# Centring only ahead of the first transposes, rstd folded in behind them, and new orders for all engines of a retention and mixture-of-experts layer

## The reference

```python
def _layernorm(x, axis=-1, eps=1e-05):
    m = jnp.mean(x, axis=axis, keepdims=True)
    v = jnp.var(x, axis=axis, keepdims=True)
    return (x - m) / jnp.sqrt(v + eps)
# attention of x = _layernorm(x)
q = (x @ Wq.T).reshape(B, T, H, dk)
k = (x @ Wk.T).reshape(B, T, H, dk)
q, k = _apply_rotary(q, k)
v = jnp.transpose((x @ Wv.T).reshape(B, T, H, dv), (0, 2, 1, 3))
scores = jnp.einsum('bhtd,bhsd->bhts', q * dk ** (-0.5), k) * decay_mask[None]
o = jnp.transpose(jnp.einsum('bhts,bhsd->bhtd', scores, v), (0, 2, 1, 3))
rms = jax.lax.rsqrt(jnp.mean(o * o, axis=-1, keepdims=True) + EPS)
g = (x @ Wg.T).reshape(B, T, H, dv)
x = x0 + (o * rms * g_norm_w * (g * jax.nn.sigmoid(g))).reshape(B, T, H * dv) @ Wo.T
# experts, of xf = _layernorm(x) in rows
shared = jax.nn.silu(xf @ sh_up_w + sh_up_b) @ sh_down_w + sh_down_b
comb = top-2 softmax weights of xf @ gate_w.T, scaled to sum to one
h = jax.nn.silu(jnp.einsum('nd,edh->neh', xf, up_w) + up_b)
y = jnp.einsum('ned,ne->nd', jnp.einsum('neh,ehd->ned', h, down_w) + down_b, comb)
return x + y + shared
```

## Time and profile before

| | us |
|---|---|
| median of 3 runs | 142.51 (142.03 to 142.53) |
| the profiled execution | 142.45 |
| its span in the profile | 140.7 |
| TensorE busy in it | 130.8 (93%) |
| VectorE busy | 104.2 (74%) |
| ScalarE busy | 78.6 (56%) |
| GpSimd busy | 48.8 (35%) |

### The profile page before, as it was taken

The page is one execution under the profiler, slowest core; times in us unless marked ns, Lnnn a source line. Parts: engine busy times, 40 slices in busy tenths (PEclk is TensorE's granted clock), DMA queues, the critical chain, the costliest instruction groups (busy, mean ns, idle before and its releaser), DMA issues.

```text
span 140.7 us, 3363 instructions
## 1 busy us (share of the span) xinstructions
PE 130.8 (93%) x1249; PEld 103.7 (74%) x1249; DVE 104.2 (74%) x311; ACT 78.6 (56%) x138; POOL 48.8 (35%) x69
## 2 busy tenths in 40 slices
PE   5659899899999999999998999999999999999990
PEld 5549799798978988886885675776557655589990
DVE  3589999989689997998796949679443982113983
ACT  4223937955562478555659762697745864471130
POOL 5458897937372342815222804502000000000000
PEclk9977999999999999999999999999999999999999
DMA  4999910000000000097000097010197200002002
GB/s 113 296 274 317 334 68 0 5 0 5 0 5 0 2 5 0 17 320 270 2 5 0 16 317 270 2 56 19 47 276 283 75 2 0 0 0 79 0 0 75
DMA packets 8659, 12.50 MB, mean 89 GB/s; under 512 B 1298, under 2 KB 5676, under 8 KB 8644
## 3 DMA queue, kind: packets, MB, share of 16 engines
q1 hardware_dynamic: 8356, 12.10, 26.7%
q10 hardware_dynamic: 288, 0.20, 0.4%
HBM read 11.20 MB, written 1.10 MB: 87 GB/s over the span
## 4 chain that ended last, share of the span: by engine, by line
PE 72%; DVE 10%; DMA 5%; SPq 4%; ACT 3%; issue 3%; DVEq 0%
PE bY L1238 17%; PE bU L1061 8%; PE bU L1062 7%; PE bU L1063 7%; DMA UW<-upw 5%; PE bA L1135 5%; PE bA L1211 4%; PE bU L1154 3%; PE bA L1129 3%; PE bA L1105 2%; PE bM L1154 2%; PE bU L1145 2%; PE bM L1180 1%; DVE SC L724 1%; SPq L267 1%
## 5 line engine op out<-in xcount | busy, mean ns | idle before, releaser
L497 ACT ACTIVATE HB<-bU,UB 128x512 f32<-128x512 f32 x36 | 24.3, 686 | 22.0 <-PE bU L1063 21.7
L1238 PE MATMUL bY<-HG,DW 128*128 128x512 f32 x48 | 24.5, 594 | 0.0
L848 DVE TENSOR_TENSOR HG<-CB,HB 128x512 f32<-128x512 f32 x24 | 16.3, 688 | 10.9 <-ACT HB L497 10.2
L353 POOL TENSOR_TENSOR RR<-SS,NHALF 128x8 f32<-128x8 f32 x8 | 13.5, 1684 | 25.9 <-DVE SS L743 25.9
L1061 PE MATMUL bU<-XH,UWH 128*128 128x512 f32 x36 | 21.5, 597 | 0.0
L1062 PE MATMUL bU<-XL,UWH 128*128 128x512 f32 x36 | 14.2, 395 | 0.0
L1063 PE MATMUL bU<-XH,UWL 128*128 128x512 f32 x36 | 14.2, 393 | 0.0
L1061 PEld LDWEIGHTS bU<-XH,UWH 128*128 128x128 f32 x36 | 6.8, 189 | 5.5 <-issue 4.3
L1238 PEld LDWEIGHTS bY<-HG,DW 128*128 128x128 f32 x48 | 8.4, 190 | 2.5 <-issue 1.4
L724 DVE TENSOR_TENSOR SC<-bA,MASK 128x512 f32<-128x512 f32 x16 | 10.2, 679 | 0.0
L1062 PEld LDWEIGHTS bU<-XL,UWH 128*128 128x128 f32 x36 | 6.8, 190 | 3.4 <-issue 3.4
(11 more groups left out here) (180 smaller groups left out, 317.8 us busy)
## 6 DMA issues: line engine op xcount, KB each, us to landing
CB<-scratch SPq DMA_DIRECT2D x12, 512.0 KB, 5.8
ROT<-rotary_tables SPq DMA_DIRECT2D x8, 256.0 KB, 4.5
out<-OUT SPq DMA_DIRECT2D x8, 128.0 KB, 1.8
X<-x SPq DMA_DIRECT2D x7, 128.0 KB, 6.1
UW<-upw SPq DMA_DIRECT2D x1, 576.0 KB, 6.6
DW<-dnw SPq DMA_DIRECT2D x1, 576.0 KB, 5.5
W<-wqkvg SPq DMA_DIRECT2D x1, 256.0 KB, 3.7
W<-wqkvg ACTq DMA_DIRECT2D x1, 128.0 KB, 3.9
```

The costliest lines, as they stand in the source:

```text
L353: pool.tensor_tensor(RR[:, n], SS[:, n], NHALF[:, 0:2 * H], ALU.pow).then_inc(rr.sem, 1)
L497: act.activation(HB[:, k, :], bU[(g * (E + 1) + k) % 2][:, :], ACT.Silu, bias=UB[:, e:e + 1]).then_inc(hid.sem, 1)
L848: dve.tensor_tensor(HG[:, k % RING, :], CB[:, k - 1, :], HB[:, k, :], ALU.mult).then_inc(gated.sem, 1)
L1238: pe.matmul(bY[:, :], DW[:, e * P:(e + 1) * P], HB[:, 0, :] if k == 0 else HG[:, k % RING, :], start=(k == 0), stop=(k == E)).then_inc(dow ...
```

## The change

For the first two pairs VectorE's `center1` subtracts the mean only, and rstd, a factor of each row of q, k, v and gate alike, comes in behind the projections: as a scale in `values` and `gates` (ScalarE, now in two halves for these pairs), and in `rotary` and `rotate` as fused instructions with three operands (VectorE, two for each product). `NORM1` goes from 4 to 2, so the pairs of group 1 are normalised on ScalarE and need `x1_bias`. The `rotate` of the first two groups and `low_w(1)`, the low half of the V and gate weights, move from GpSimd to VectorE. The V and gate weights are loaded by ScalarE's queue behind the Q and K weights, no longer by SP's queue ahead of x, and one load of x moves ahead of the constants. Ten warm-up matmuls become seven and two, in another bank. The lists of all engines and the banks in `PLACE` are new; the sets of steps in them are otherwise the same. The diff, cut to these edits and to the first part of each list (and the last part of TensorE's):

```diff
@@ -40,22 +40,23 @@
 SLOTS = 4
 TABLES = 6
 
-NORM1, NORM2 = 4, 4
+NORM1, NORM2 = 2, 4
+
+FOLD = 2
 
...
@@ -267,13 +268,12 @@
                 sp.dma_start(dst, rotary_tables[n // 2, :, c]).then_inc(ld_rot[n].sem, 16)
 
             load_first_x(sp, 0)
-            sp.dma_start(W[:, QK:], wqkvg[:, QK:]).then_inc(ld_w[1].sem, 16)
             load_x(sp, 1)
             load_rotary(0)
             load_x(sp, 2)
             load_rotary(1)
+            load_x(sp, 3)
             sp.dma_start(CN[:, :], const).then_inc(ld_c.sem, 16)
-            load_x(sp, 3)
             load_rotary(2)
             load_rotary(3)
...
 
             rstd1(0, 0)
             rstd1(0, 1)
-            low_w(1)
             rstd1(1, 0)
             rstd1(1, 1)
             fold_norm()
-            rotate(0, 0)
             low_experts()
-            rotate(0, 1)
             rstd1(2, 0)
             rstd1(2, 1)
-            rotate(1, 0)
-            rotate(1, 1)
+            rms(0, 0)
             rstd1(3, 0)
-            rms(0, 0)
+            normalize_out(0, 0)
             rstd1(3, 1)
-            normalize_out(0, 0)
...
             load_first_x(act, 1)
             act.dma_start(W[:, 0:QK], wqkvg[:, 0:QK]).then_inc(ld_w[0].sem, 16)
+            act.dma_start(W[:, QK:], wqkvg[:, QK:]).then_inc(ld_w[1].sem, 16)
...
             def x1_norm(g, p):
-                act.wait_ge(nm1.sem, pair(g, p) - NORM1 + 1)
+                act.wait_ge(nm1.sem, pair(g, p) - max(NORM1, FOLD) + 1)
...
             def values(g, p):
                 act.wait_ge(v_ps.sem, v_ps.at(g, p))
-                act.copy(V[:, slot(g, p)].rearrange("r b n -> r (b n)"), place("proj_v", g, p)).then_inc(v_sb.sem, 1)
+                if pair(g, p) < FOLD:
+                    act.wait_ge(rs1.sem, rs1.at(g, p))
+                    for b in range(2):
+                        last = act.activation(V[:, slot(g, p), b], place("proj_v", g, p)[:, b * HV:(b + 1) * HV], ACT.Identity,
+                                              scale=RS1[:, 2 * pair(g, p) + b:2 * pair(g, p) + b + 1])
+                else:
+                    last = act.copy(V[:, slot(g, p)].rearrange("r b n -> r (b n)"), place("proj_v", g, p))
+                last.then_inc(v_sb.sem, 1)
 
             def gates(g, p):
                 act.wait_ge(g_ps.sem, g_ps.at(g, p))
                 if pair(g, p) >= SLOTS:
                     act.wait_ge(ogr.sem, ogr.at(*back(g, p, SLOTS)))
-                act.activation(SG[:, slot(g, p)].rearrange("r b n -> r (b n)"), place("proj_g", g, p), ACT.Silu).then_inc(sg.sem, 1)
+                if pair(g, p) < FOLD:
+                    act.wait_ge(rs1.sem, rs1.at(g, p))
+                    for b in range(2):
+                        last = act.activation(SG[:, slot(g, p), b], place("proj_g", g, p)[:, b * HV:(b + 1) * HV], ACT.Silu,
+                                              scale=RS1[:, 2 * pair(g, p) + b:2 * pair(g, p) + b + 1])
+                else:
+                    last = act.activation(SG[:, slot(g, p)].rearrange("r b n -> r (b n)"), place("proj_g", g, p), ACT.Silu)
+                last.then_inc(sg.sem, 1)
...
             split_w(0)
+            x1_hi(0, 0)
             split_w(1)
-            x1_hi(0, 0)
             x1_hi(0, 1)
             gates(0, 0)
+            gates(0, 1)
+            x1_norm(1, 0)
+            values(0, 0)
+            values(0, 1)
+            qk_sb(0, 0)
+            x1_hi(1, 0)
             split_experts()
-            gates(0, 1)
-            values(0, 0)
-            x1_hi(1, 0)
-            values(0, 1)
+            x1_norm(1, 1)
+            qk_sb(0, 1)
+            split_biases()
+            gates(1, 0)
             x1_hi(1, 1)
-            split_biases()
-            qk_sb(0, 0)
-            gates(1, 0)
+            squares(0, 0)
+            values(1, 0)
+            x1_norm(2, 0)
+            values(1, 1)
+            qk_sb(1, 0)
+            x1_norm(2, 1)
             gates(1, 1)
-            qk_sb(0, 1)
...
+            def center1(g, p):
+                dve.wait_ge(mv1.sem, mv1.at(g, p))
+                for b in range(2):
+                    t = g * TILES + 2 * p + b
+                    last = dve.tensor_scalar(XN1[:, g % 2, (2 * p + b) * P:(2 * p + b + 1) * P], X[:, t * P:(t + 1) * P],
+                                             MV1[:, t, 0:1], None, ALU.subtract)
+                last.then_inc(xn1.sem, 1)
...
-                dve.tensor_tensor(RA[:, p], src.rearrange("r (b n) -> r b n", b=2), cos.unsqueeze(1).to_broadcast([P, 2, QK]),
-                                  ALU.mult)
+                if pair(g, p) < FOLD:
+                    dve.wait_ge(rs1.sem, rs1.at(g, p))
+                    for b in range(2):
+                        t = 2 * pair(g, p) + b
+                        dve.scalar_tensor_tensor(out=RA[:, p, b], in0=src[:, b * QK:(b + 1) * QK], scalar=RS1[:, t:t + 1], in1=cos,
+                                                 op0=ALU.mult, op1=ALU.mult)
+                else:
+                    dve.tensor_tensor(RA[:, p], src.rearrange("r (b n) -> r b n", b=2),
+                                      cos.unsqueeze(1).to_broadcast([P, 2, QK]), ALU.mult)
...
             def rotate(g, p):
                 dve.wait_ge(rparts.sem, rparts.at(g, p))
+                if pair(g, p) < FOLD:
+                    for b in range(2):
+                        t = 2 * pair(g, p) + b
+                        last = dve.scalar_tensor_tensor(out=QKR[:, slot(g, p), b], in0=RB[:, p, b], scalar=RS1[:, t:t + 1],
+                                                        in1=RA[:, p, b], op0=ALU.mult, op1=ALU.add)
+                    last.then_inc(rot.sem, 1)
+                    return
...
             stats1(0, 0)
+            center1(0, 0)
             stats1(0, 1)
+            center1(0, 1)
+            x1_lo(0, 0)
             low_w(0)
-            normalize1(0, 0)
-            normalize1(0, 1)
-            x1_lo(0, 0)
+            low_w(1)
+            x1_lo(0, 1)
             stats1(1, 0)
-            x1_lo(0, 1)
+            rotary(0, 0)
+            x1_bias(1, 0)
             stats1(1, 1)
-            rotary(0, 0)
-            normalize1(1, 0)
-            normalize1(1, 1)
+            rotate(0, 0)
             rotary(0, 1)
+            state(0, 0)
+            rotate(0, 1)
             x1_lo(1, 0)
+            x1_bias(1, 1)
             stats1(2, 0)
+            masked(0, 0)
+            rotary(1, 0)
+            stats1(2, 1)
             x1_lo(1, 1)
-            state(0, 0)
-            stats1(2, 1)
-            rotary(1, 0)
-            masked(0, 0)
+            rotate(1, 0)
+            x1_bias(2, 0)
+            gate_out(0, 0)
+            mean_squares(0, 0)
+            x1_bias(2, 1)
+            state(0, 1)
+            stats1(3, 0)
+            masked(0, 1)
+            state(1, 0)
+            stats1(3, 1)
+            x1_lo(2, 0)
...
-                    pe.matmul(bY[:, 0:P], IDN[:, :], IDN[:, :], start=True, stop=True)
+                    pe.matmul(bA[:, 3, 0:P], IDN[:, :], IDN[:, :], start=True, stop=True)
...
             pe.wait_ge(idn.sem, 1)
-            keep_busy(10)
+            keep_busy(7)
             x1_t(0, 0)
+            keep_busy(2)
             x1_t(0, 1)
+            after(xl1, 0, 0)
             proj_qk(0, 0)
             proj_g(0, 0)
             after(xl1, 0, 1)
+            proj_g(0, 1)
             proj_qk(0, 1)
-            proj_g(0, 1)
+            after(rparts, 0, 0)
             proj_v(0, 0)
-            after(xl1, 0, 0)
+            after(sg, 0, 1)
+            proj_v(0, 1)
+            after(sg, 0, 0)
+            qk_t(0, 0)
+            after(v_sb, 0, 0)
+            state_add(0, 0)
             x1_t(1, 0)
-            proj_v(0, 1)
-            after(sg, 0, 1)
+            after(rparts, 0, 1)
+            scores(0, 0)
+            after(qkt, 0, 0)
+            qk_t(0, 1)
+            after(st, 0, 0)
+            proj_qk(1, 0)
+            after(v_sb, 0, 1)
+            proj_g(1, 0)
+            after(qkt, 0, 1)
             x1_t(1, 1)
-            qk_t(0, 0)
-            after(v_sb, 0, 1)
-            state_add(0, 0)
-            after(rparts, 0, 1)
-            proj_qk(1, 0)
+            attend(0, 0)
+            after(rparts, 1, 0)
+            proj_v(1, 0)
+            after(sg, 1, 0)
+            state_add(0, 1)
             after(xl1, 1, 1)
-            proj_g(1, 0)
-            after(v_sb, 0, 0)
-            after(sg, 0, 0)
-            scores(0, 0)
-            after(st, 0, 0)
-            proj_qk(1, 1)
-            after(rparts, 1, 0)
-            proj_g(1, 1)
-            after(sg, 1, 0)
-            qk_t(0, 1)
-            after(xl1, 1, 0)
-            state_add(0, 1)
-            attend(0, 0)
-            after(rparts, 1, 1)
-            proj_v(1, 0)
-            after(qkt, 0, 1)
             proj_v(1, 1)
-            after(sg, 1, 1)
+            after(v_sb, 1, 0)
             qk_t(1, 0)
-            after(st, 0, 1)
-            x1_t(2, 0)
...
             down_last(3, 1)
```

(11 more changed lines are left out.)

510 lines of the change are left out of this document (244 added, 266 removed), and 23 rows, old and new, of the table PLACE.

## The result

The changed kernel takes 138.70 us (median of 4 runs, 138.29 to 139.15), the kernel before 142.27 us beside it (141.86 to 142.53): a ratio of 0.975, 95% interval 0.971 to 0.980, so 3.6 us less where 1.9 were forecast. The profiled execution took 138.97 us with a span of 137.2, against 142.45 and 140.7 before. In all that follows a median takes in every execution, and a ratio leaves out those more than 1.5% above the fastest of their kernel.

The account below looks back on a forecast made before the run. VectorE and TensorE were taken to bind the attention part together. TensorE's lead of 3.0 us less a router 1.1 us later gave a gain of 1.9: 142.45 - 1.9 = 140.55 us, range 138.4 to 142.6.

Parts of the forecast that it names:

- The start: Front of the run: first projection at 6.9 us instead of 9.36, 2.4 us sooner, between 1.9 and 3.0.
- W came earlier: V and gate weights' load on ScalarE's queue: seen at 7.5 us, between 6.8 and 8.4; VectorE waits 1.25 us.
- The path to the first router: VectorE up to x2_lo(0, 1): net 5.0 us more work, there at 48.2 us; TensorE's router 1.1 us later.
- Other idle time, about 3 us: VectorE's remaining waits ahead of the first router: left unchanged, as no row says the new order has less.
- the recovered clock: TensorE's clock at the front: not counted again, since TensorE there waits for VectorE and not its own pace.
- The stretched instructions of VectorE beside GpSimd: Ahead of the first router: four normalisations and two tiny biases lose their waits beside GpSimd, 2.0 us back.
- TensorE's lead: At the first router: net 3.0 us of matmul work already issued that lay behind it before.
- new idle time: TensorE behind the router, where combine weights return by DMA: counted at nothing; its appearance would show the forecast wrong.
- The tail: End of the run: two up-projections move between down-projections, same matmuls in all; nothing, within 0.2 us.
- TensorE sets the pace, W early: Rival for the front: W seen at 6.8 us saves 0.7, less idle time 1.5 more; 138.35 us, chance 0.23.
- W late and the clock low: Rival for the front: W seen at 8.4 us, TensorE's clock falls, first projections at half rate; 142.1 us, chance 0.20.
- VectorE's new instructions stand behind GpSimd: Rival: VectorE's added SBUF instructions meet GpSimd's long ones, three or four meetings cost 3.5 us; 144.05 us, chance 0.12.

Follow-up runs that it names:

- e5: The changed kernel itself, run again unchanged beside other runs on the same chip: 138.89 us, ratio 0.976 to the kernel before.
- e7: Changed kernel with the V and gate weights' load back second on SyncE's queue: 138.48 us, ratio 0.975 to the kernel before.
- e1: Changed kernel without its nine warm-up matmuls: 139.77 us, ratio 0.980 to the kernel before.
- e4: Changed kernel with its orders, but first two pairs fully normalised by VectorE and V and gate weights loaded as before: 141.00 us, ratio 0.988 to the kernel before.
- e13: Orders alone (old normalisation and loads) with nine warm-up matmuls for seven and five for two: 139.46 us, ratio 0.980 to the kernel before.
- e2: Kernel before with twelve warm-up matmuls for ten and three more between the first two pairs' transposes: 142.22 us, ratio 0.999.
- e11: Changed kernel with rotations of pairs (1, 0) and (1, 1) and low half of V and gate weights back on GpSimd: 140.61 us, ratio 0.990 to kernel before.
- e8: Changed kernel with values(3, 1) moved ahead of transposed_out(2, 0) in ScalarE's order: 138.03 us, ratio 0.970 to the kernel before.
- e6: Changed kernel with first two pairs normalised by VectorE again, its orders and loads kept: 140.79 us, ratio 0.988 to the kernel before.
- e3: Kernel before with only the centring and later rstd for the first two pairs, their rotations on VectorE: 144.87 us, ratio 1.018.
- e10: As e3, with ScalarE's cast of the experts' up weights moved behind the high half of pair (1, 0): 142.93 us, ratio 1.002 to the kernel before.
- e9: Orders alone (old normalisation and loads) with five warm-up matmuls for two behind the first transposes: 140.29 us, ratio 0.983 to the kernel before.

## Why the prediction was right and wrong

**The start was right.** First projection 6.94 us (forecast 6.9), x for pair (0, 1) at 4.84 (4.9), low half of the first pair at 6.04 (6.2), no stretched centring. That x landed so close to the forecast is in part chance: in e5, the same kernel, its statistics start at 4.40 without a wait, and with W back on SyncE's queue (e7) x came at 5.01, 0.17 later, where the sum of the queue's bytes had up to 1.2.

**W came earlier than I took it**, seen at 6.86 us, at the lower of my two bounds (6.8) and not at 7.5, and VectorE's wait was 0.73 us and not 1.25. The shares of the two queues from 4.5 to 5.5 us in the changed kernel:

```profile
q10 hardware_dynamic: 96, 0.18, 54.7%
q1 hardware_dynamic: 105, 0.12, 44.3%
```

With rows of 2 KB ScalarE's queue got the larger share, where with rows of 1 KB it had 24.1% against 68.0. The Trainium skill (DMA: Bandwidth & Descriptors, section Queues, rings and completion order) says that each DMA engine takes turns between the queues, a packet at a time. The counts here agree, 96 packets against 105; those before don't, 90 against 296, and no run tells why. The load itself, by e7, decides nothing.

**The path to the first router is the step that failed, and with it the idle time on that path.** The sum went along VectorE, to which it gave "Other idle time, about 3 us, I leave as it is", let "TensorE's router" start at about 48.4 us behind it, and left the clock out: "the recovered clock isn't counted again, since at the front TensorE now waits for VectorE and not for its own pace". The router started at 46.85 us, 0.2 sooner than before (its first matmul was at 47.03 there) where the sum had 1.1 later. In VectorE's terms: from the first low half to the end of x2_lo(0, 1) it was busy for 34.91 of 37.75 us before and for 37.31 of 39.71 after. Its work grew by 2.4 us where the sum had 5.0 - 2.0 = 3.0. Its idle time fell from 2.84 to 2.40 us where the sum let it grow to 4.1. With the start 0.16 sooner that is the 2.45 us by which x2_lo(0, 1) ended before my 48.2 (0.16 + 0.6 + 1.7). Of the 1.7 us of idle time, 0.5 are W. The other 1.2 are small waits that are gone, above all three for ScalarE's high halves (0.67 us) and most of one for GpSimd (0.65, now 0.26).

Why they could go is in TensorE's rows: from 14.80 us on it waits for nothing until 56.91, so VectorE no longer sets the pace there, and its idle time is what TensorE's pace leaves it. Whatever slows TensorE ahead of that point then counts, the clock too: low, it costs the changed kernel 1.2 us in its trace (e1) and the orders alone 1.4 (e4 against e13). I had argued that the two engines bind the middle of the run together and that TensorE waits for VectorE at the front; in the old orders a faster TensorE does only wait longer (e2), though for ScalarE. The clock belonged into the sum as a condition of the orders.

**The stretched instructions of VectorE beside GpSimd**, which I gave back at 2.0 us, are gone. What they cost in the old orders no run shows. In the new ones, putting work back on GpSimd costs 1.4 us (e11) with one instruction stretched, by 0.8 us, and mostly since GpSimd's results come late.

**TensorE's lead** was 3.0 us in the sum; from the router's first matmul to the end it is 3.3 (93.7 us before, 90.4 after), so this term was right. The 2.6 of the table count from the low half; without the new wait at 56 us they are 3.6 (e8). I expected new idle time, if any, where the combine weights come back by DMA; it came from ScalarE's queue, where a table load of 1.28 us and two activations stand ahead of a copy.

**The tail** was taken as no difference. The time from the low half to the end is the same in all kernels of one order, but no run changes the tail's order alone, so this isn't shown.

**The rivals.** "TensorE sets the pace, W early" (138.35 us) had the time within 0.4 us, W's landing, and 1.5 us of idle time saved where 1.2 were; its mechanism is the one that the runs show, with the clock as the part it lacked. "W late and the clock low" didn't occur; e1 shows that the clock costs 1.2 us in it. "VectorE's new instructions stand behind GpSimd" didn't occur: no such meeting is in the trace. What the three parts are worth, in steps of the medians: the orders 142.3 to 141.0 (e4), the clock to 139.5 (e13), fold and loads together to 138.8. With the clock up the fold's own part is small (0.4 us at the low half in e6's trace). Without the fold and without more warm-up the median is 1.9 us longer (e6), while in every trace with new orders, fold and warm-up TensorE is at 2.4 GHz by 7.8 us. That keeping the clock up is the fold's main use is likely by this, not shown: e6 has one trace.

Open: why the clock stays up in e6's profiled execution and falls in e4's, with TensorE idle for 1.14 and 1.54 us ahead of the same transposes; and whether the spread of executions of e1, e3, e4, e6, e7 and e10 is the clock's. Each has one trace only. The mean granted clock of each execution doesn't settle it: e6's fastest has 0.994 and its next three 0.983 to 0.986, but its two slowest 0.999 and 1.000. The Trainium skill (TensorE: Matmul & The Clock Gate, section Part 1: The HAM clock gate) says that the point at which the clock changes differs from run to run of one kernel. The two traces of the changed kernel agree: in the one the matmuls run at 2.4 GHz from the first projection at 6.94 us, in the other (e5) they run at 1.2 GHz until 7.3, with the same warm-up before.

## What to carry to other kernels

Find the point from which one engine no longer waits, and sum up to there, along that engine: here TensorE ran without a wait from 15 us on, and the start of one instruction behind it told the end to 0.1 us in the traces of all thirteen kernels with the new orders, once the one wait that e8 removes is allowed for. Before you count an engine's idle time as given, ask what feeds it and at which clock; an engine that seems to set the pace can be waiting, in small pieces, for one whose clock is low. An earlier start is worth nothing by itself in an in-order queue: look for the first entry that waits for a load and for who stands behind it (e3), and for idle time just ahead of a late copy (e8).

## What the runs showed of the hardware

The profile's granted clock stood at 1.00 from the first instruction in e1, while the matmuls there ran in steps of 0.21 us until 12.3 us, as they do at a clock of 0.50 in e4; the steps are the safer sign at the start of a run. An unbroken stretch of work didn't always bring 2.4 GHz by the first projection: in e9 TensorE stood for 0.73 us, worked without a break from 5.69 us and still ran at 1.2 GHz until 10.8; in e6, after 0.55 us of standing at the same place, it was at 2.4 GHz by the first projection at 8.70, and in e4, after 0.56, at 1.2 GHz. Whether the length of the wait matters no run shows.
